# Turning the experts' operands by transposing DMAs instead of by TensorE, in an attention and mixture-of-experts kernel

## The reference, cut to what matters

```python
scores = softmax(xf @ gate_w.T)
_, sel = top_k(scores + expert_bias, 2)          # 2 of 8 experts for each token
top_scores = take_along_axis(scores, sel, 1)
routed = xf[token_idx] * top_scores_sorted[:, None]
h = silu(xe @ w1[e]) * (xe @ w3[e])              # 256 -> 704, twice
out = out + h @ w2[e] * m                        # 704 -> 256
out = zeros_like(xf).at[token_idx].add(routed_out)
x = x + out
```

## Time and profile before

| | |
|---|---|
| median of 3 runs | 493.14 us (491.72 to 495.26) |
| the profiled execution | 496.29 us, span 494.5 us |
| PE busy, of the span | 83% |
| DVE / ACT / POOL busy | 54% / 39% / 45% |
| mean granted TensorE clock | 0.898 of full speed |

### The profile page before, as it was taken

The page is one execution under the profiler, slowest core; times in us unless marked ns, Lnnn a source line. Parts: engine busy times, 40 slices in busy tenths (PEclk is TensorE's granted clock), DMA queues, the critical chain, the costliest instruction groups (busy, mean ns, idle before and its releaser), DMA issues.

```text
span 494.5 us, 10564 instructions
## 1 busy us (share of the span) xinstructions
PE 410.3 (83%) x2969; PEld 310.3 (63%) x2970; DVE 267.1 (54%) x635; ACT 195.1 (39%) x351; POOL 222.7 (45%) x281
## 2 busy tenths in 40 slices
PE   4826998999998840148999999999999999999970
PEld 3613787877786730126777777777777777777740
DVE  2756566667674259824555555555555555555530
ACT  2256576686675344003333332333333333333310
POOL 5376355544446449032444444444444444444321
PEclk9877799999997655559999999999999999999985
DMA  6821343333263533010222222222222222232215
GB/s 201 267 90 61 100 165 116 103 111 90 97 191 112 179 109 95 1 33 13 44 44 43 36 40 40 37 43 43 43 43 42 33 43 36 39 43 43 33 21 180
DMA packets 29299, 38.35 MB, mean 78 GB/s; under 512 B 5205, under 2 KB 23906, under 8 KB 29250
## 3 DMA queue, kind: packets, MB, share of 16 engines
q1 hardware_dynamic: 21472, 27.60, 17.7%
q0 software_dynamic: 7488, 10.39, 13.1%
q10 hardware_dynamic: 322, 0.15, 0.1%
HBM read 28.62 MB, written 11.60 MB: 81 GB/s over the span
## 4 chain that ended last, share of the span: by engine, by line
PE 75%; DVE 8%; issue 4%; POOL 4%; ACT 3%; DMA 3%; POOLq 0%; SPq 0%; DVEq 0%; ACTq 0%
PE sc L1334 10%; PE sc L1335 10%; PE sc L1336 10%; PE ptps L1324 6%; PE bank L1357 6%; PE bank L1353 5%; PE bank L1199 5%; PE bank L1355 4%; PE bank L1268 3%; PE ptps L1244 3%; POOL w_lo L490 2%; PE bank L1306 2%; ACT w_hi L591 2%; PE bank L1257 1%; DMA w_hi<-n_L_xattn_in_proj_weight 1%
## 5 line engine op out<-in xcount | busy, mean ns | idle before, releaser
L567 POOL DMA_INDIRECT acc<-arena,put_now x39 | 62.5, 1603 | 113.4 <-DVE arena L1076 113.4
L1334 PE MATMUL sc<-w_hi,arena 128*128 x312 | 98.6, 316 | 1.0 <-DVE arena L1054 1.0
L1335 PE MATMUL sc<-w_hi,arena 128*128 x312 | 98.6, 316 | 0.0
L1336 PE MATMUL sc<-w_lo,arena 128*128 x312 | 98.5, 316 | 0.0
L490 POOL TENSOR_TENSOR w_lo<-stage_w,w_hi 128x1408 f16<-128x1408 f32 (+3 forms) x32 | 71.7, 2256 | 46.2 <-ACT w_hi L591 46.2
L1066 DVE SCALAR_TENSOR_TENSOR arena<-sc,slot_score,arena 128x352 f32<-128x352 f32 (+1 forms) x117 | 53.0, 481 | 66.9 <-ACT arena L735 66.9
L735 ACT ACTIVATE arena<-sc,slot_score 128x352 f32<-128x352 f32 x78 | 43.1, 553 | 90.6 <-PE sc L1336 90.6
L1353 PE MATMUL bank<-w_hi,arena 128*128 x234 | 64.1, 274 | 2.2 <-DVE arena L1081 2.2
L742 ACT ACTIVATE arena<-ptps 128x768 f16<-128x768 f32 x39 | 31.6, 810 | 83.5 <-PE ptps L1324 83.5
L1357 PE MATMUL bank<-w_lo,arena 128*128 x234 | 64.5, 275 | 0.0
L1079 DVE TENSOR_TENSOR arena<-ptps,arena 128x640 f16<-128x640 f32 x39 | 32.2, 824 | 44.4 <-ACT arena L742 44.4
(11 more groups left out here) (196 smaller groups left out, 714.0 us busy)
## 6 DMA issues: line engine op xcount, KB each, us to landing
stage_w<-in_L_ffn_w SPq DMA_DIRECT2D x16, 704.0 KB, 4.4
stage_w<-in_L_ffn_w SPq DMA_DIRECT2D x16, 256.0 KB, 2.9
stage_w<-in_L_ffn_w SPq DMA_DIRECT2D x32, 64.0 KB, 2.8
acc<-arena SPq DMA_DIRECT2D x16, 128.0 KB, 1.7
table<-xn SPq DMA_DIRECT2D x16, 128.0 KB, 1.8
arena<-in_x SPq DMA_DIRECT2D x2, 896.0 KB, 6.3
arena<-table,get_now POOLq DMA_INDIRECT x39, 2.8
acc<-arena,put_now POOLq DMA_INDIRECT x39, 3.8
```

The source lines that it names most:

```text
L567: pool.indirect_dma_start(out=acc[:, :], out_offset=bass.IndirectOffsetOnAxis(ap=put_now[q][:, 0:1], axis=0), in_=y_sb[q], in_offset=None, ...
L1334: pe.matmul(ps[:, c, :], gT_hi[par][:, kk], w_hi[:, cols], start=k == 0, stop=False)
L1335: pe.matmul(ps[:, c, :], gT_lo[par][:, kk], w_hi[:, cols], start=False, stop=False)
L1336: ins = pe.matmul(ps[:, c, :], gT_hi[par][:, kk], w_lo[:, cols], start=False, stop=k == KD - 1)
```

## The change

The split into hi and lo now comes before the transposition. ACT and DVE write hi and lo of the gathered rows side by side, 128 x 512 float16 (`x16`), and hi and lo of the inner tile side by side, 128 x 1408 float16 (`hid16`), both in SBUF with tokens on the partitions. SP turns each by one transposing DMA from SBUF to SBUF: `gT`, four squares of 128 x 128, and `hT`, eleven squares. The eight transposes on PE per tile, and their two PSUM areas, are gone. The down projection of tile j moves from step j+1 to step j+2, after the up projection of that step; the last down projection reads all 128 rows of the array (64 of hi, 64 of lo) in both of its matmuls. The gather of a tile is issued one step earlier, since it needs to be split and turned, and its buffer is free once it is split. On SP, step j first issues the transposition of the rows of tile j+2, then that of the inner tile of j. The loop has three steps written out before and six behind it.

```diff
+            def rows_across(j, par):
+                sp.wait_ge(s["x16_hi"], j + 1)
...
+                sp.wait_ge(s["x16_lo"], j + 1)
...
+                if not isinstance(j, int) or j >= 2:
+                    sp.wait_ge(s["h_ps"], 2 * (j - 1))
...
+                sp.dma_start_transpose(gT[par], x16[par]).then_inc(gt_in[par], 16)
+            rows_across(0, 0)
+            rows_across(1, 1)
+            def step(j, par):
...
+                    rows_across(j + 2, par)
...
+                    sp.wait_ge(s["h16_hi"], j + 1)
+                    sp.wait_ge(s["h16_lo"], 3 * (j + 1))
+                    if not static or j >= 2:
+                        sp.wait_ge(s["y_ps"], j - 1)
+                    sp.dma_start_transpose(hT[par], hid16[par]).then_inc(ht_in[par], 16)
# POOL
-                if not static or j + 2 < J:
-                    pool.wait_ge(s["gt_ps"], j + 1)
-                    pool.wait_ge(s["sc_tmp"], j + 1)
-                    gather(j + 2, par, not static)
+                if not static or j + 3 < J:
+                    rows_split(j + 1)
+                    gather(j + 3, 1 - par, not static)
+                if not static or j >= 2:
...
+                    pool.wait_ge(s["y_ready"], j - 1)
+                    if not static or j >= 3:
+                        pool.wait_ge(s["put_done"], 16 * (j - 2))
# ACT
-                act.activation(gT_hi[par], bk6[:, 0:KD * P], ACT.Copy).then_inc(s["gt_hi"], 1)
+                act.wait_ge(gathered[par], landed(j, par))
+                act.activation(x16[par][:, 0:D], gx[par][:, 0:D], ACT.Copy).then_inc(s["x16_hi"], 1)
...
-                    act.activation(hT_hi[par], hT_ps, ACT.Copy).then_inc(s["ht_hi"], 1)
+                    act.activation(hid16[par][:, 0:F], sil[par], ACT.Copy).then_inc(s["h16_hi"], 1)
# DVE
+                    if not static or j + 2 < J:
+                        slots(j + 2, par)
+                    dve.wait_ge(s["h16_hi"], j + 1)
+                    for a, b, at in ((LC, F, F), (0, FH, KF * P), (FH, LC, KF * P + FH)):
+                        dve.tensor_tensor(hid16[par][:, at:at + b - a], sil[par][:, a:b], hid16[par][:, a:b], ALU.subtract)\
+                            .then_inc(s["h16_lo"], 1)
+                if not static or j >= 2:
+                    dve.wait_ge(s["y_ps"], j - 1)
...
+                    dve.tensor_copy(y_sb[par], bk7[:, 0:D]).then_inc(s["y_ready"], 1)
# PE
-                    for c in range(KF):
-                        ins = pe.transpose(hT_ps[:, c * P:(c + 1) * P], hid[q][:, c * P:(c + 1) * P], idt)
-                    ins.then_inc(s["ht_ps"], 1)
+                    pe.wait_ge(gt_in[par], landed(j, par))
                     for c in range(2):
+                        if not static or j >= 1:
+                            pe.wait_ge(s["h_ready"], 2 * j - 1 + c)
...
-                if not static or j + 1 < J:
-                    x_rows(j + 1, q, 16 * ((j + 1 - q) // 2 + 1) if static else 8 * (j + 1 - q) + 16)
-                if not static or j >= 1:
+                if not static or j >= 2:
...
+                    pe.wait_ge(ht_in[par], landed(j - 2, par))
```

More of the change, by code:

```diff
@@ L127, in xattn_moe @@
         LC = (KF - 1) * P
-        hid = [take(KF * P) for _ in range(2)]
         sil = [take(F) for _ in range(2)]
-        hT_hi = [take(KF * P, F16) for _ in range(2)]
-        hT_lo = [take(LC, F16) for _ in range(2)]
-        y_sb = [take(D) for _ in range(2)]
+        hid16 = [take(2 * F, F16) for _ in range(2)]
         gx = [take(XR) for _ in range(2)]
-        gT_hi = [take(KD * P, F16) for _ in range(2)]
-        gT_lo = [take(KD * P, F16) for _ in range(2)]
+        hT = [take(2 * F, F16).rearrange("p (c t) -> p c t", t=P) for _ in range(2)]
+        gT = [take(2 * KD * P, F16).rearrange("p (c t) -> p c t", t=P) for _ in range(2)]
+        assert 2 * F == (2 * KF - 1) * P
         assert take.at <= T * D + T * E * E + 2 * T * TOPK * E + J * E
+        x16 = [xn[i][:, :].bitcast(F16) for i in range(2)]
+        y_sb = [xn2[i][:, :] for i in range(2)]
         score_w = sb("score_w", [P, E])
@@ L235, in xattn_moe, with landed @@
         gathered = [s["gat0"], s["gat1"]]
+        gt_in = [s["gt_in0"], s["gt_in1"]]
+        ht_in = [s["ht_in0"], s["ht_in1"]]
+        def landed(j, par):
+            return 16 * ((j - par) // 2 + 1) if isinstance(j, int) else 8 * (j - par) + 16
         def back(u, par, k):
@@ L297, in expert_steps @@
                 step(j, j % 2)
-            with eng.Fori(1, (J - 3) // 2) as v:
+            with eng.Fori(1, (J - 5) // 2) as v:
                 step(2 * v + 1, 1)
                 step(2 * v + 2, 0)
-            for j in range(J - 2, J + 1):
+            for j in range(J - 4, J + 2):
                 step(j, j % 2)
         def carry(eng):
-            eng.sem_inc(s["carried_dve" if eng.engine == nc.vector.engine else "carried_pool"], 1)
+            names = {nc.vector.engine: "carried_dve", nc.gpsimd.engine: "carried_pool", nc.sync.engine: "carried_sp"}
+            eng.sem_inc(s[names[eng.engine]], 1)
         def v_bank(b):
@@ L407, in _ @@
                              r_small[0][:, b:T:2, :]).then_inc(s["score_st"], 16)
+            def rows_across(j, par):
+                sp.wait_ge(s["x16_hi"], j + 1)
+                carry(sp)
+                sp.wait_ge(s["x16_lo"], j + 1)
+                carry(sp)
+                if not isinstance(j, int) or j >= 2:
+                    sp.wait_ge(s["h_ps"], 2 * (j - 1))
+                    carry(sp)
+                sp.dma_start_transpose(gT[par], x16[par]).then_inc(gt_in[par], 16)
+            rows_across(0, 0)
+            rows_across(1, 1)
+            def step(j, par):
+                static = isinstance(j, int)
+                if not static or j + 2 < J:
+                    rows_across(j + 2, par)
+                if not static or j < J:
+                    sp.wait_ge(s["h16_hi"], j + 1)
+                    carry(sp)
+                    sp.wait_ge(s["h16_lo"], 3 * (j + 1))
+                    carry(sp)
+                    if not static or j >= 2:
+                        sp.wait_ge(s["y_ps"], j - 1)
+                        carry(sp)
+                    sp.dma_start_transpose(hT[par], hid16[par]).then_inc(ht_in[par], 16)
+            expert_steps(sp, step)
             sp.wait_ge(s["put_done"], 16 * J)
@@ L720, in rows_high @@
             def rows_high(j, par):
[L722 to L725 removed]
+                act.wait_ge(gathered[par], landed(j, par))
+                act.activation(x16[par][:, 0:D], gx[par][:, 0:D], ACT.Copy).then_inc(s["x16_hi"], 1)
             rows_high(0, 0)
+            rows_high(1, 1)
             def step(j, par):
@@ L736, in step @@
                                        scale=slot_score[par][:, 0:1]).then_inc(s["silu_done"], 1)
-                    if not static or j + 1 < J:
-                        rows_high(j + 1, 1 - par)
-                    act.wait_ge(s["ht_ps"], j + 1)
+                    if not static or j + 2 < J:
+                        rows_high(j + 2, par)
+                    act.wait_ge(s["h_ready"], 2 * (j + 1))
                     if not static or j >= 2:
-                        act.wait_ge(s["y_ps"], j - 1)
-                    act.activation(hT_hi[par], hT_ps, ACT.Copy).then_inc(s["ht_hi"], 1)
+                        act.wait_ge(ht_in[par], landed(j - 2, par))
+                    act.activation(hid16[par][:, 0:F], sil[par], ACT.Copy).then_inc(s["h16_hi"], 1)
             expert_steps(act, step)
@@ L1045, in slots @@
                 static = isinstance(j, int)
-                dve.wait_ge(gathered[par], 16 * ((j - par) // 2 + 1) if static else 8 * (j - par) + 16)
+                dve.wait_ge(gathered[par], landed(j, par))
                 oh = tile_oh[:, j, :] if static else tile_oh[:, bass.ds(j, 1), :].rearrange("p u e -> p (u e)")
-                if not static or j >= 1:
-                    dve.wait_ge(s["sc_ready"], j)
                 dve.tensor_tensor(score_w[:, :], gx[par][:, D:XR], oh, ALU.mult).then_inc(s["sc_tmp"], 1)
@@ L1060, in step @@
                 if not static or j < J:
-                    for a, b, at in ((0, FH, 0), (FH, F, FH), (LC, F, F)):
-                        c = a // FH
+                    for c in range(2):
+                        cc = slice(c * FH, (c + 1) * FH)
                         dve.wait_ge(s["silu_done"], 2 * j + c + 1)
-                        dve.scalar_tensor_tensor(out=hid[par][:, at:at + b - a], in0=h3_ps[:, c, a - c * FH:b - c * FH],
-                                                 scalar=slot_score[par][:, 0:1], in1=sil[par][:, a:b],
-                                                 op0=ALU.mult, op1=ALU.mult).then_inc(s["h_ready"], 1)
@@ L1069, in step @@
[L1069 to L1082, removed]
+                        dve.scalar_tensor_tensor(out=sil[par][:, cc], in0=h3_ps[:, c, :], scalar=slot_score[par][:, 0:1],
```

(27 more changed lines are left out.)

47 lines of the change are left out of this document (21 added, 26 removed).

## The result

The changed kernel took 461.52 us in the median of 4 runs (461.0 to 462.03), against 492.81 us before: a ratio of 0.936, with a 95% interval from 0.932 to 0.940. The forecast was 455, range 450 to 530; the way and the bound were right, the time came out 6.5 us above the point.

A forecast was written before the change was run, and what follows sets the result against it. PE's own work bounds the kernel; 39 steps of 5.54 (216.1) plus 2.5, 3.5, 1.8 and 1.0 give 224.9 in place of 262.8, so 458.4 profiled, 455 us on the median's scale; range 450 to 530.

The forecast's parts named there:

- 1.03 us per tile: PE's transposes per tile, 0.22 for gathered rows and 0.81 for the inner tile, which the change removes.
- Bare PE work of 5.44: PE's work left per step: 3.58 of up projection and 1.86 of down projection, in us.
- The seam: PE's loss from two new waits per step: nothing to 0.10 us, taken as 0.10, making the step 5.54.
- The DMA engines' work: Transposing pieces at 18 ns, 2.15 us per step; with gather and scatter 3.8 of 5.54, off the path.
- The rule that speaks against the change: If 1309 ns were paid per square in turn, fifteen squares cost 19.6 us per step, and the time is 1005.
- The ways of the rows and of the inner tile: From up projection's end: rows issued +2.2, wanted +7.5, landing 1.8; inner tile issued +3.5, wanted +11.1, landing 3.7 us.
- Rival B: Scatter and gather land later on busier DMA engines; scatters landing in 5.0 make the step 6.0, time 473; chance 21%.
- the sum: 262.8 us before becomes 224.9 from first matmul to last down projection, 37.9 less; profiled execution 496.29 becomes 458.4.
- the 1.8 for a low clock in the last 17 matmuls: At the stage's end, the last 17 matmuls may all run at the low clock level: +1.8 us.
- the 3.5 of the forecast: At the end PE idles +3.5 us for the last inner tile, landing 7.2 after its up projection.
- The start: Before the first matmul, first rows need 0.37 + 0.42 + 1.8 and gaps in place of 1.7: +1.0 us.
- the scatter's 4.8: POOL's scatter waits for the one before: 3.8 to landing plus 1.0 to the start, against a 5.54 step.

The follow-up runs named there:

- b1: The kernel before with only one of the inner tile's six transposes left on PE: 472.31 us.
- e1: The changed kernel with only six of the inner tile's eleven squares turned: 461.46 us.
- g1: The changed kernel with the scatters of the odd tiles replaced by a 1 KB write to an unused buffer: 459.32 us.
- f2: As f1, with PE loading the next tile's weight offset between the halves of the up projection, one load per tile in place of two: 453.49 us.
- e3: The changed kernel with PE's program alone written out for all 41 steps, no loop: 460.06 us.
- f1: As e3, with DVE copying the finished rows of j-2 ahead of the lo pieces of tile j: 458.35 us.
- e4: The changed kernel with the inner tile of j issued on SP ahead of the rows of j+2: 494.46 us.
- e2: The changed kernel with SP turning eleven more squares per step, from the expert weights into an unread buffer: 477.85 us.

## Why the prediction was right, and where it missed

**PE bounds the kernel before, and 1.03 us per tile go: right.** b1 shows it for the kernel before, and in the kernel after e1 and g1 rule out the DMA engines and the scatters as the bound. Bare PE work of 5.44 was right to the hundredth, as f2 shows.

**The seam: too small.** I took 0.10 per step; in mid-stage the changed kernel lost 0.17 (mean 5.61). It is PE's own sequencer, with the loop and the loads of the weight offset, and not a landing: e3 brought 5.61 to 5.52, and f2, with the loads moved, 5.49 (f1) to 5.45. In the kernel before the transposes, which need no offset, stood behind that load. Whether they hid it was not tried: the 0.15 that b1 found at that place, beyond 0.11 for each transpose, is of the same size.

**The DMA engines' work: right.** 18 ns a piece forecast, 20.3 measured; 0.69 of the step forecast, 0.77 measured. That the price came so near is in part luck: it was taken in proportion to bytes between two plain transfers, at 7.7 and 65 ns, and no row had told that a transposing piece lies on that line. The rule that speaks against the change (the Trainium skill, "VectorE: DVE Perf Modes", "The three transpose paths", 1309 ns for a bf16 square of 128 x 128) doesn't hold as a price per square here: fifteen squares in a step of 5.6 us leave at most 0.37 us for each. No run turned a single square by itself; the stage's first transposition, of four squares, landed 2.56 after its issue. The other page, "Advanced Engine Details and Errata" of the Trainium skill, section "X-Bar Transpose (TRN2)", has transposing DMAs as fast as regular ones and comes nearer, without being met: those four squares, 128 KB, took 2.56 to land, where a plain store of 128 KB took 1.8.

**The ways of the rows and of the inner tile: right in kind, the rows' margin too wide.** I gave the rows 1.8 to land, from a plain store; alone they took 2.56, behind the tile in e4 3.48. The tile's 3.7, put together from a store and a load, was met: 3.6 in e4 and 3.7 in g1 in the median. From the forecast's own numbers, the two transfers landing one after the other in the other order put the rows at 3.5 + 3.7 + 1.8 = 9.0, past the 7.5 that they have; I had that sum at hand and did not make it when I expected e4 to be free. In the changed kernel the rows' round is far from binding only because of the order on SP.

**Rival B: not in mid-stage.** Scatters landed in 4.0 (3.8 before) and waited for each other in 4 of 39 cases.

**The step of the sum that failed is its end.** The forecast of 458.4 stands against 461.81 for the profiled execution. From the first matmul to the end of the last it had 223.9, and 224.9 were measured. That this is off by 1.0 only is partly luck, for two errors cancel: from 227.84 to 429.63 the 36 steps lost some 6 against 5.44 each, where the forecast had 3.9 for all seams, and the 1.8 for a low clock in the last 17 matmuls did not come. After pauses of 1.82 and 1.51 of PE they ran at the full granted clock:

```profile
440.50:442.70 2.20, 2.03 (x17) 1.58 (x17) 0.04 (x1) 0.00 (x0) 0.00 (x0) 1.00 0.21 30
```

The first two up projections lost 2.9 where 2.5 was put, and the pauses at the end are near the 3.5 of the forecast. The start had +1.0, and from landed rows to the first matmul 3.64 (214.12 to 217.76) against 1.69 before are +1.95, 0.95 more. Behind the last matmul it had nothing, and 3.7 were added: the last three down projections follow each other in less than the scatter's 4.8, so their scatters queue up. I checked that chain against a step of 5.54 and left out that the end has no steps of 5.54. That makes 1.0 + 0.95 + 3.7 = 5.7; the part ahead of the experts, some 2.2 shorter in this execution, took as much of it back and leaves about the 3.4 that were missed. The other 3.1 of the 6.5 are in the scale and in rounding: I took off the 3.15 by which the profiled execution stood above the median before, and after it stands 0.3 above (461.81 and 461.52); 455.25 was rounded to 455.

These are the rows of the start, with the landing told by the first score row of DVE:

```profile
214.12 0.17 DVE L1091 TENSOR_TENSOR score_w<-arena 128x8 f32<-128x8 f32 x1 [3.40 <-DMA arena<-table,get_now]
...
217.76 0.47 PE L1353 MATMUL sc<-w_hi,arena 128*128 x1 [8.86 <-DMA arena<-xn]
```

## What to carry to other kernels

When the bound engine does work that only moves data, another path can take it over at its own speed as long as each result has more time than it takes to land; count that time over the whole round (here two steps), from the wait that starts the transfer to the use, and for every order on the queue that issues it: the same transfers in the other order gave the whole 31 us back. And check a serial chain not only against the steady step but also against the end, where work that was deferred comes bunched.

## What the runs showed of the hardware that was not expected

- One issue of a transposing DMA holds SP for 1.19 us with 4 squares, 1.21 with 6 (e1) and 1.39 with 11, where a plain store's issue took about 0.34. In e2, with the share of the DMA engines at 1.09, the last of three issues of a step took 2.02 for eleven squares.
- While SP's queue moved transposing pieces in one stretch of 3 us, the queue of the gathers and scatters moved 44 packets of 2023. The scatters' landing grew from 3.8 to 4.0 with the share of the DMA engines at 0.77, and to 5.1 in e2 at 1.09; but it was 4.3 in e4 at 0.68, so the share alone does not give it.
- A float32 transpose of 128 x 128 on PE costs 0.11 among its like (b1).
- On PE's sequencer the load of an offset from SBUF and the address arithmetic behind it are not free at the head of a step: with them moved into the up projection the mean step was 5.45 and not 5.49 (f1).
